# Four blocks on one core: merged attention weights in the third, projections in three rounded terms, joined rows, and a new order

## The chip, the cores and the metric

One core of a Trainium2 chip runs the whole program. The metric is device time in microseconds (us) of one execution.

## The reference

The program computes four blocks in a row on an activation of 2048 tokens by 256 channels, handled as four batches of 512 tokens. Each block normalises its input and adds two branches to it:

```python
xn = _layernorm(x); x = x + L0_attn(xn) + L0_ffn(xn)   # causal attention, 16 heads of 16; ternary feed-forward, 1024 units
xn = _layernorm(x); x = x + L1_attn(xn) + L1_ffn(xn)   # gated recurrence; 16 experts by top 2 with slots, and a shared expert of 176
xn = _layernorm(x); x = x + L2_attn(xn) + L2_ffn(xn)   # attention, one head of 256; spline-coded feed-forward, 1024 units
xn = _layernorm(x); x = x + L3_attn(xn) + L3_ffn(xn)   # attention with rope, 16 heads; 8 experts in bf16, shared expert of 176, plus xn

q = x@wq.T; k = x@wk.T; v = x@wv.T                     # L2_attn
out = softmax(q@k.T / sqrt(256)) @ v @ wo.T
logits = x @ gate_w.T                                  # L1_ffn, 16 columns; L3_ffn has the same with router_w, 8 columns
shared = (act(x@Ws1.T) * (x@Ws3.T)) @ Ws2.T            # L1_ffn and L3_ffn, act is silu and sigmoid
```

## The kernel before, in words

The code numbers the blocks k = 0 to 3. A batch b has four token tiles of 128. Every matrix product runs on TensorE (PE) into PSUM: three pairs of banks used in a ring ("pair") and two single banks.

Every engine executes its own list of steps in an order that is written out by hand. `PARTS` names the steps of each engine, `DUE` gives each step a turn, and `Turns` sorts by turn. Nothing is reordered while the program runs: a step that waits holds up all later steps of its engine. `freed` (L485) makes PE wait, before it fills a bank, until the readers named in `FREED` are done with what was in it.

Products come in three kinds. Plain fp32 operands are issued by PE as two matmul records each, so the counts of the trace are twice those of the code. Operands rounded to fp32r take one record; the feed-forward layers of blocks 0 and 2 use these with a high part and a low part that sum to the fp32 value (`cut_high`, `cut_low`, `h_high`, `h_low`, `w_in2`, `w_out2`). Block 3's experts run in bf16.

A batch of a block starts with the layer norm (`stat`, `norm` on VectorE, DVE), eight transposes (`turn_x`, L618), and a copy of the result from PSUM by ScalarE, ACT (`turned`, L1520: to `xnT`, in blocks 0 and 2 also rounded to `cut_high`; `cut_low` on DVE, L1029, subtracts that). Blocks 0 and 3 then project a token tile in one step, `qkv` (L627): two fp32 products of 512 columns, two of 256. Head groups follow: `fold`, `score`, `top` (row maxima on DVE), `refold`, `prob`, `exp` (ACT), `weigh`, with feed-forward steps between them in the hand-written order. Block 1 projects with `proj`, computes gates, a scan and two group norms mostly on DVE, and routes with `logit` (L825), `route_a` to `route_e` and `count`; its experts follow. Block 2 is `qk2` (L872, queries and keys apart), `v2`, `score2`, `probs_turn`, `weigh2` (L904, probabilities times values), and the output product with `wo2` in `out` (L715), where the feed-forward sum joins. Block 3's router is `vote` (L912). `shared` (L815) computes the gate and up columns of the shared expert in two steps, the 128 first and the 48 last columns, each with two products per half. At the start, twelve chunks of ternary weights are made by ACT, PE, DVE and GpSimd (POOL) in turn (`tern_*`). Between blocks 1 and 2 the spline weights are made (`cubic`, `spline`, `spline_sum`). Loads are issued by SyncE (SP) in the order of `load`. `quarter` (L983) scales the query weights and bias of blocks 0 and 3 by 0.25.

## Time and profile before

| what | value |
|---|---|
| device time, median of 3 runs | 1569.27 us (1563.61 to 1571.36) |
| the profiled execution: its time / its span | 1562.3 us / 1561.0 us |
| PE busy, share of the span | 1336.0 us, 86% |
| DVE busy | 946.1 us, 61% |
| ACT busy | 680.3 us, 44% |
| POOL busy | 412.9 us, 26% |
| mean granted clock of TensorE | 0.91 of full |

The profile is one execution. Busy time is the time that an engine spent in instructions; a clock of 1.00 is 2.4 GHz and 0.50 is 1.2 GHz. The duration of one matmul includes its way through the array, so the pace of a row of matmuls is read from the distance between starts.

### The profile page before, as it was taken

How to read it: one execution, taken by the hardware profiler on the slowest of the kernel's cores; microseconds unless marked ns; L12 is line 12 of the kernel's file. 1: busy time of each engine (PE TensorE's matmuls, PEld its weight loads, DVE VectorE, ACT ScalarE, POOL GpSimd, SP SyncE). 2: the span in 40 equal slices, each digit the busy share in tenths (PEclk: the TensorE clock that was granted, in tenths of full speed). 3: DMA queues.
4: the chain of work that ended last, by engine and by line, in shares of the span. 5: the costliest groups of instructions: out<-in, count | busy, mean ns of one | idle time of the engine just before them, and what ended most of it. 6: DMA issues, size and time to landing. Idle time of an engine off the chain costs nothing.

```text
span 1561.0 us, 19705 instructions
## 1 busy us (share of the span) xinstructions
PE 1336.0 (86%) x7705; PEld 810.8 (52%) x7716; DVE 946.1 (61%) x1822; ACT 680.3 (44%) x960; POOL 412.9 (26%) x397
## 2 busy tenths in 40 slices
PE   0589999999999668889469999999899898988997
PEld 0367666776654335445146677676445335434434
DVE  5895563584557999882586234346675765556560
ACT  3435555444664755442024224231463453453452
POOL 2465000541002331410662122133223302301300
PEclk9979996899999889899579999999799899989978
DMA  7000000004010000025550000000311000200100
GB/s 227 14 1 1 1 2 1 1 1 150 22 45 28 27 24 4 27 75 165 155 81 0 1 1 1 8 17 1 61 42 38 17 0 1 54 1 1 55 1 14
DMA packets 32012, 53.21 MB, mean 34 GB/s; under 512 B 5200, under 2 KB 19760, under 8 KB 31280
## 3 DMA queue, kind: packets, MB, share of 16 engines
q1 hardware_dynamic: 27840, 40.99, 8.5%
q0 software_dynamic: 4080, 10.97, 3.3%
q8 instruction: 61, 1.00, 0.3%
q14 instruction: 31, 0.25, 0.1%
HBM read 43.99 MB, written 10.52 MB: 35 GB/s over the span
## 4 chain that ended last, share of the span: by engine, by line
PE 45%; DVE 27%; issue 15%; ACT 5%; POOL 5%; DMA 1%; SPq 1%; DVEq 0%; POOLq 0%; ACTq 0%
PE pair L609 15%; PE bank L609 14%; DVE max L1094 6%; PE bank L692 4%; PE pair L680 3%; PE pair L642 3%; ACT probs L1580 2%; PE pair L660 2%; POOL cos L1885 1%; DVE xn L1026 1%; POOL square_sum L1902 1%; POOL gathered L1934 1%; DMA gathered<-outbox,slots 1%; SPq L1966 1%; DVE tern_mask L973 1%
## 5 line engine op out<-in xcount | busy, mean ns | idle before, releaser
L1094 DVE TENSOR_REDUCE max<-pair 128x2 f32<-128x1024 f32 (+3 forms) x256 | 245.9, 1015 | 85.3 <-PE pair L650 51.9
L1580 ACT ACTIVATE probs<-pair 128x1024 f32<-128x1024 f32 (+3 forms) x256 | 206.9, 871 | 128.9 <-PE pair L650 78.3
L1892 POOL TENSOR_TENSOR h_low<-hidden,h_high 128x512 fp32r<-128x512 f32 x64 | 82.4, 1288 | 262.3 <-ACT h_high L1615 262.3
L692 PE MATMUL bank<-probs,v 128*32 128x512 f32 (+3 forms) x1024 | 131.4, 590 | 2.5 <-ACT probs L1580 2.2
L680 PE MATMUL pair<-qs,ks 52*128 52x512 f32 (+3 forms) x512 | 110.8, 480 | 24.1 <-DVE max L1094 13.1
L660 PE MATMUL pair<-ks,qs 50*128 50x512 f32 (+3 forms) x512 | 115.9, 480 | 16.9 <-DVE max L1094 7.0
L680 PEld LDWEIGHTS pair<-qs,ks 52*128 52x128 f32 x512 | 50.5, 207 | 106.7 <-issue 37.0
L609 PE MATMUL pair<-wqk,xnT 128*128 128x512 f32 x192 | 98.3, 637 | 3.0 <-DVE tern_what L981 2.6
L1144 DVE SCALAR_TENSOR_TENSOR hidden<-hidden,pair 128x512 f32<-128x512 f32 x64 | 43.7, 683 | 82.5 <-ACT hidden L1607 82.5
L1952 POOL TENSOR_TENSOR h<-mix_h,h 128x512 bf16<-128x512 f32 x48 | 55.4, 1168 | 133.8 <-DMA h<-comb 78.8
L660 PEld LDWEIGHTS pair<-ks,qs 50*128 50x128 f32 x512 | 52.3, 205 | 71.1 <-DVE max L1094 30.8
L1607 ACT ACTIVATE hidden<-pair 128x512 f32<-128x512 f32 x64 | 38.2, 597 | 106.3 <-PE pair L609 106.0
L1127 DVE TENSOR_TENSOR x<-bank,x 128x512 f32<-128x512 f32 x32 | 21.9, 686 | 101.3 <-PE bank L609 101.3
L609 PE MATMUL bank<-wo,rowsT 128*128 128x256 f32 x256 | 70.7, 405 | 10.2 <-DVE x L1127 2.4
L642 PE MATMUL pair<-ident_r,stack 128*128 128x128 f32 x512 | 57.3, 272 | 13.2 <-POOL stack L1861 9.1
L1615 ACT CAST h_high<-hidden 128x512 fp32r<-128x512 f32 x64 | 39.4, 619 | 66.6 <-DVE hidden L1146 52.5
L1857 POOL CAST stack<-raw 128x256 fp32r<-128x256 f32 x32 | 13.8, 430 | 201.7 <-DVE stack L1085 201.7
L642 PEld LDWEIGHTS pair<-ident_r,stack 128*128 128x128 f32 x512 | 51.7, 151 | 24.2 <-issue 14.5
L609 PEld LDWEIGHTS bank<-wo,rowsT 128*128 128x128 f32 x256 | 46.1, 196 | 26.8 <-issue 8.6
L609 PE MATMUL pair<-xnT,shared_in 128*48 128x512 f32 (+1 forms) x128 | 59.7, 612 | 0.1
L1563 ACT CAST qs<-pair 128x1024 fp32r<-128x1024 f32 x32 | 32.5, 1017 | 56.9 <-PE pair L642 56.8
L609 PE MATMUL pair<-x,w_in 128*128 128x512 bf16 x181 | 51.6, 426 | 6.0 <-DVE mix_h L1494 3.1
(293 smaller groups left out, 2823.8 us busy)
## 6 DMA issues: line engine op xcount, KB each, us to landing
expert_in<-in_experts_in SPq DMA_DIRECT2D x16, 352.0 KB, 3.8
expert_out<-in_experts_out SPq DMA_DIRECT2D x16, 256.0 KB, 5.1
h<-comb SPq DMA_DIRECT2D x4, 1024.0 KB, 5.0
x<-in_x SPq DMA_DIRECT2D x4, 512.0 KB, 11.2
wqk<-in_wqk SPq DMA_DIRECT2D x4, 512.0 KB, 3.9
tern_raw<-in_ffn_in SPq DMA_DIRECT2D x8, 256.0 KB, 6.5
inbox<-zeros SPq DMA_DIRECT2D x4, 512.0 KB, 5.3
tokens<-inbox SPq DMA_DIRECT2D x16, 128.0 KB, 2.5
```

The lines of the kernel that those rows point to most:

```text
L609: made = mm(out, lhsT, rhs, start=start and n == 0, stop=stop and n == len(pairs) - 1)
L642: made = turn(to[:, p, tt * P:(tt + 1) * P].bitcast(F32R), m.stack[g % 2][:, tt, half, 2 * p:2 * p + 2, :].rearrange("p h r -> p (h r)"), ...
L660: made = mm(to[:, hh, 0:n], m.qs[g % 2][r0:r0 + AUG + 2, p, qt * P:(qt + 1) * P], m.ks[g % 2][r0:r0 + AUG + 2, p, 0:n], start=True, stop=k ...
L680: made = mm(to[:, hh, q0:T], m.ks[g % 2][r0:r0 + AUG + 4, p, kt * P:(kt + 1) * P], m.qs[g % 2][r0:r0 + AUG + 4, p, q0:T], start=True, stop ...
L692: made = mm(to[32 * j:32 * j + 32, q0:T], m.v[b % 2][:, kt, G * g + j, :], m.probs[(2 * kt + j // 2) % 4][:, j % 2, q0:T], start=kt == 0, ...
L1094: V.tensor_reduce(m.max[:, g % 2, qt, 2 * p:2 * p + 2], to[:, :, 0:n], AX.X, ALU.max).then_inc(*s.done("top"))
L1144: V.scalar_tensor_tensor(h[:, :], h[:, :], 1.0, to[:, 0, :], ALU.add, ALU.mult).then_inc(*dve.up())
L1580: A.activation(m.probs[(2 * kt + p) % 4][:, :, q0:T], to[:, :, q0:T], ACT.Exp).then_inc(*s.done("exp"))
L1607: A.activation(m.hidden[k][j % 2][:, :], to[:, 0, :], ACT.Tanh, scale=0.5).then_inc(*s.done("tanh"))
L1615: A.copy(m.h_high[k][:, j, :], m.hidden[k][j % 2][:, :]).then_inc(*s.done("high"))
L1892: Q.tensor_tensor(m.h_low[k][:, j, :], m.hidden[k][j % 2][:, :], m.h_high[k][:, j, :].bitcast(F32), ALU.subtract).then_inc(*s.done("low"))
L1952: Q.tensor_tensor(m.h16[:, j, :], m.mix_h[j % 2][:, :], m.h16[:, j, :], ALU.mult).then_inc(*s.done("mix_comb"))
```

## The change

- Block 2 (the third): the host hands over the four raw weight matrices. Two new PE steps `merge` multiply wq by wk and wv by wo once; ACT and DVE split each result into a high and a low part. `qk2` becomes one step for a batch, a product of the input with the merged matrix, and `score2` multiplies it with the input itself. `v2` uses the other merged matrix. `weigh2`, `weighed2` and the product with wo are gone; `out` multiplies the probabilities with `v2` directly.
- Three rounded terms (`three`: high·high, low·high, high·low) replace each fp32 product in `qkv` of blocks 0 and 3, `qk2`, `v2`, `score2`, and `shared` of block 3. New steps `split_high` (ACT) and `split_low` (POOL) split the weights. Block 3 now has a `cut_low` too, and its `x16` copy is part of `turned`.
- `shared` in both blocks: the 48 last gate and up columns sit in one product of 112 columns instead of two of 48.
- `logit` and `vote` are gone: the router's 16 or 8 columns are added to the value projection (272 or 264 columns), with a small copy to SBUF by ACT (block 1) or DVE (block 3).
- `quarter` is gone; the factor 0.25 moves into `exp` (ACT's scale), and the host scales `k_extra` by 4.
- Nearly all turns in `DUE` are new, among them those of the loads, and several tiles lie elsewhere in SBUF.

The diff, cut to its core (`layout` on the host, most turn lists and addresses are left out):

```diff
-    "score2": "639 644 645 653 656 659 663 667 688 693 694 701 706 711 712 717",
+    "score2": "638 634 639 644 661 662 657 666 686 687 683 679 705 710 706 701",
...
-    "load": "0 1 3 2 5 6 7 4 8 17 23 24 33 35 34 76 77 9 83 82 84 85",
+    "load": "1 7 6 0 5 2 8 4 9 17 23 24 33 34 35 76 3 81 82 83 84",
...
-    "turn": lambda k, b: [("turned", (k, b))] + [("cut_low", (k, b))] * (k in (0, 2)),
+    "turn": lambda k, b: [("turned", (k, b))] + [("cut_low", (k, b))] * (k != 1),
...
+    "merge": lambda i: [("merge_high", (i,)), ("merge_low", (i,))],
+    "qk2": lambda b: [("qk2_out", (b,)), ("qk2_low", (b,))],
...
+    def three(x, w):
+
+        return [(x[0], w[0]), (x[1], w[0]), (x[0], w[1])]
...
     def qkv(k, b, tt):
         to = bank("qkv", k, b, tt)
-        pe.wait_ge(*at("turned", k, b))
-        pe.wait_ge(*s.loaded(f"qkv{k}"))
-        pe.wait_ge(*at("quarter", k))
-        xT = [m.turned(k, b)[:, kc, tt * P:(tt + 1) * P] for kc in range(KC)]
-        products(to[:, 0, :], [(xT[kc], m.wqk[k][:, kc, :]) for kc in range(KC)])
-        products(to[:, 1, 0:C], [(xT[kc], m.wv[k][:, kc, :]) for kc in range(KC)]).then_inc(*s.done("qkv"))
+        pe.wait_ge(*at("cut_low", k, b))
+        pe.wait_ge(*at("split_high", k // 3))
+        pe.wait_ge(*at("split_low", k // 3))
+        for part, high, low in ((0, m.wqk_high[k], m.wqk_low[k]), (1, m.wv_high[k], m.wv_low[k])):
+            pairs = [pair for kc in range(KC) for pair in three([x[:, kc, tt * P:(tt + 1) * P] for x in (m.high(k, b), m.cut_low)], [high[:, kc, :], low[:, kc, :]])]
+            made = products(to[:, part, 0:low.shape[2]], pairs)
+        made.then_inc(*s.done("qkv"))
...
-            pe.wait_ge(*at("weighed2", b))
+            pe.wait_ge(*s.last("v2_out", [(b, half) for half in PAIRS]))
+            pe.wait_ge(*s.last("probs_out", [(b, 2 * i + n) for n in PAIRS]))
...
-            made = products(to[:, cols], [(m.rowsT[k][:, kc, tok], m.wo[k][:, kc, :]) for kc in range(KC)], stop=k == 0)
+            if k == 2:
+                products(to[:, cols], [(m.probsT[:, kt, tok], m.v2[b % 2][:, kt, :]) for kt in range(TT)], stop=False)
+            else:
+                made = products(to[:, cols], [(m.rowsT[k][:, kc, tok], m.wo[k][:, kc, :]) for kc in range(KC)], stop=k == 0)
...
-        products(to[:, 1, 0:C], [(xT[kc], m.wv1[:, kc, :]) for kc in range(KC)]).then_inc(*s.done("proj"))
+        products(to[:, 1, 0:C + E1], [(xT[kc], m.wv1[:, kc, :]) for kc in range(KC)]).then_inc(*s.done("proj"))
...
     def shared(k, b, c):
         to = bank("shared", k, b, c)
-        pe.wait_ge(*at("turned", k, b))
-        pe.wait_ge(*s.loaded("rest1" if k == 1 else "shared3"))
-        n_rows = (P, I - P)[c]
-        for part in PAIRS:
-            c0 = part * I + c * P
-            made = products(to[0:n_rows, part, :], [(m.shared_in[k][:, kc, c0:c0 + n_rows], m.turned(k, b)[:, kc, :]) for kc in range(KC)])
+        if k == 1:
+            pe.wait_ge(*at("turned", k, b))
+            pe.wait_ge(*s.loaded("rest1"))
+        else:
+            pe.wait_ge(*at("cut_low", k, b))
+            pe.wait_ge(*at("split_high", 2))
+            pe.wait_ge(*at("split_low", 2))
+        for part, cols in enumerate(((slice(0, P), slice(P, 2 * P)), (slice(2 * P, SHARED),))[c]):
+            if k == 1:
+                pairs = [(m.shared_in[1][:, kc, cols], m.turned(b)[:, kc, :]) for kc in range(KC)]
+            else:
+                pairs = [pair for kc in range(KC) for pair in three([m.shared_high[:, kc, cols], m.shared_low[:, kc, cols]], [m.high(3, b)[:, kc, :], m.cut_low[:, kc, :]])]
+            made = products(to[0:(P, SMALL)[c], part, :], pairs)
         made.then_inc(*s.done("shared"))
-
-    def logit(b):
-        to = bank("logit", b)
-        pe.wait_ge(*at("turned", 1, b))
-        pe.wait_ge(*s.loaded("rest1"))
-        for tt in range(TT):
-            made = products(to[:, tt * E1:(tt + 1) * E1], [(m.turned(1, b)[:, kc, tt * P:(tt + 1) * P], m.wroute1[:, kc, :]) for kc in range(KC)])
-        made.then_inc(*s.done("logit"))
...
-    def qk2(b, half):
-        to = bank("qk2", b, half)
-        pe.wait_ge(*at("turned", 2, b))
+    def merge(i):
+
+        to = bank("merge", i)
         pe.wait_ge(*s.loaded("qkv2"))
         for mc in range(KC):
-            c0 = half * C + mc * P
-            made = products(to[:, mc, :], [(m.wqk[2][:, kc, c0:c0 + P], m.turned(2, b)[:, kc, :]) for kc in range(KC)])
+            made = products(to[:, mc * C:(mc + 1) * C], [(m.raw2[:, 2 * i, kc, mc * P:(mc + 1) * P], m.raw2[:, 2 * i + 1, kc, :]) for kc in range(KC)])
+        made.then_inc(*s.done("merge"))
+
+    def qk2(b):
+        to = bank("qk2", b)
+        pe.wait_ge(*at("cut_low", 2, b))
+        pe.wait_ge(*at("merge_high", 0))
+        pe.wait_ge(*at("merge_low", 0))
+        for mc in range(KC):
+            pairs = [pair for kc in range(KC) for pair in three([w[:, kc, mc * P:(mc + 1) * P] for w in m.merged[0]], [x[:, kc, :] for x in (m.cut_high, m.cut_low)])]
+            made = products(to[:, mc, :], pairs)
         made.then_inc(*s.done("qk2"))
     def v2(b, i):
         to = bank("v2", b, i)
-        pe.wait_ge(*at("turned", 2, b))
-        pe.wait_ge(*s.loaded("qkv2"))
+        pe.wait_ge(*at("cut_low", 2, b))
+        pe.wait_ge(*at("merge_high", 1))
+        pe.wait_ge(*at("merge_low", 1))
         for n in PAIRS:
             tok = slice((2 * i + n) * P, (2 * i + n + 1) * P)
-            made = products(to[:, n * C:(n + 1) * C], [(m.turned(2, b)[:, kc, tok], m.wv[2][:, kc, :]) for kc in range(KC)])
+            pairs = [pair for kc in range(KC) for pair in three([x[:, kc, tok] for x in (m.cut_high, m.cut_low)], [w[:, kc, :] for w in m.merged[1]])]
+            made = products(to[:, n * C:(n + 1) * C], pairs)
         made.then_inc(*s.done("v2"))
     def score2(b, qt):
         to = bank("score2", b, qt)
-        pe.wait_ge(*at("qk2_out", b, 0))
-        pe.wait_ge(*at("qk2_out", b, 1))
-        qk = m.qk2[b % 2]
-        products(to[:, :], [(qk[:, 0, kc, qt * P:(qt + 1) * P], qk[:, 1, kc, :]) for kc in range(KC)]).then_inc(*s.done("score2"))
+        pe.wait_ge(*at("qk2_out", b))
+        pe.wait_ge(*at("qk2_low", b))
+        pairs = [pair for kc in range(KC) for pair in three([q[:, kc, qt * P:(qt + 1) * P] for q in m.qk2[b % 2]], [x[:, kc, :] for x in (m.cut_high, m.cut_low)])]
+        products(to[:, :], pairs).then_inc(*s.done("score2"))
...
-    def quarter(k):
-        dve.wait_ge(*s.loaded(f"bias{k}"))
-        dve.wait_ge(*s.loaded(f"qkv{k}"))
-        V.tensor_scalar(m.bias[k][:, 0, :], m.bias[k][:, 0, :], 0.25, None, ALU.mult).then_inc(*dve.up())
-        V.tensor_scalar(m.wqk[k][:, :, 0:C], m.wqk[k][:, :, 0:C], 0.25, None, ALU.mult).then_inc(*s.done("quarter"))
...
         to = bank("turn", k, b)
         dve.wait_ge(*at("turned", k, b))
-        V.tensor_tensor(m.cut_low[:, :, :], to[:, :, :], m.cut_high[:, :, :].bitcast(F32), ALU.subtract).then_inc(*s.done("cut_low"))
+        if k == 3 and b == 0:
+            dve.wait_ge(*s.last("unit", [(2, BATCH - 1, j) for j in range(UNITS)]))
+            dve.wait_ge(*s.last("score2", [(BATCH - 1, qt) for qt in range(TT)]))
+            dve.wait_ge(*s.last("v2", [(BATCH - 1, i) for i in PAIRS]))
+        elif k == 3:
+            dve.wait_ge(*s.last("qkv", [(3, b - 1, tt) for tt in range(TT)]))
+            dve.wait_ge(*s.last("shared", [(3, b - 1, c) for c in PAIRS]))
+        V.tensor_tensor(m.cut_low[:, :, :], to[:, :, :], m.high(k, b).bitcast(F32), ALU.subtract).then_inc(*s.done("cut_low"))
...
+    def merge_low(i):
+        to = bank("merge", i)
+        dve.wait_ge(*at("merge_high", i))
+        V.tensor_tensor(m.merged[i][1][:, :, :], to[:, :].rearrange("p (k c) -> p k c", k=KC), m.merged[i][0][:, :, :].bitcast(F32), ALU.subtract).then_inc(*s.done("merge_low"))
+
+    def qk2_low(b):
+        to = bank("qk2", b)
+        dve.wait_ge(*at("qk2_out", b))
+        V.tensor_tensor(m.qk2[b % 2][1][:, :, :], to[:, :, :], m.qk2[b % 2][0][:, :, :].bitcast(F32), ALU.subtract).then_inc(*s.done("qk2_low"))
...
+        if k in (0, 2) and b > 0:
+            act.wait_ge(*s.last("unit", [(k, b - 1, j) for j in range(UNITS)]))
+        if k == 2 and b > 0:
+            act.wait_ge(*s.last("score2", [(b - 1, qt) for qt in range(TT)]))
+            act.wait_ge(*s.last("v2", [(b - 1, i) for i in PAIRS]))
...
+        A.copy(m.high(k, b), to[:, :, :]).then_inc(*(act.up() if k == 3 else s.done("turned")))
+        if k == 3:
             if b > 0:
-                act.wait_ge(*s.last("unit", [(k, b - 1, j) for j in range(UNITS)]))
-            elif k == 2:
-                act.wait_ge(*s.last("finish", [(b2, h, last) for b2 in B for h in PAIRS for last in PAIRS]))
-                act.wait_ge(*at("route_e", BATCH - 1))
-                for b2 in B:
-                    act.wait_ge(*s.sent(b2))
-                act.wait_ge(*s.last("weighted", [(b2, h, last) for b2 in B for h in PAIRS for last in PAIRS]))
-                act.wait_ge(*s.last("count", [(b2,) for b2 in B]))
-            A.copy(m.cut_high[:, :, :], to[:, :, :]).then_inc(*s.done("turned"))
+                act.wait_ge(*s.last("mix", [(b - 1, j) for j in range(MIX)]))
+            else:
+                act.wait_ge(*at("probs_turn", BATCH - 1, 0))
+            A.copy(m.x16[:, :, :], to[:, :, :]).then_inc(*s.done("turned"))
+
+    def split_high(n):
+
+        k = (0, 3, 3)[n]
+        act.wait_ge(*s.loaded(("qkv0", "qkv3", "shared3")[n]))
+        if n == 1:
+            act.wait_ge(*s.last("combine", [(b, tt) for b in B for tt in range(TT)]))
+        if n == 2:
+            A.copy(m.shared_high[:, :, :], m.shared_in[3][:, :, :]).then_inc(*s.done("split_high"))
+            return
+        A.copy(m.wqk_high[k][:, :, :], m.wqk[k][:, :, :]).then_inc(*act.up())
+        A.copy(m.wv_high[k][:, :, :], m.wv[k][:, :, :]).then_inc(*s.done("split_high"))
...
+    def split_low(n):
+
+        k = (0, 3, 3)[n]
+        pool.wait_ge(*at("split_high", n))
+        for w, high, low_ in ((m.shared_in[3], m.shared_high, m.shared_low),) if n == 2 else ((m.wqk[k], m.wqk_high[k], m.wqk_low[k]), (m.wv[k], m.wv_high[k], m.wv_low[k])):
+            Q.tensor_tensor(low_[:, :, :], w[:, :, :], high[:, :, :].bitcast(F32), ALU.subtract).then_inc(*(pool.up() if w.shape[2] == 2 * C else s.done("split_low")))
...
-    def weigh2(b):
...
-    def vote(b):
...
-    def weighed2(b):
...
-    def x16(b):
...
```

## Rows read from the trace of the kernel before

**Rows 1.** The page: busy us of each engine, share of the span, instructions.
```profile
PE 1336.0 (86%) x7705; PEld 810.8 (52%) x7716; DVE 946.1 (61%) x1822; ACT 680.3 (44%) x960; POOL 412.9 (26%) x397
```

**Rows 2.** Stages: stretch, length, busy PE, PEld, DVE, ACT, POOL; clock, DMA share, GB/s.
```profile
0.00:120.00 120.00, 60.55 (x296) 41.09 (x297) 96.14 (x178) 45.66 (x71) 55.69 (x55) 0.90 0.27 79
120.00:462.00 342.00, 324.46 (x2998) 225.76 (x2997) 186.27 (x349) 179.38 (x266) 77.93 (x96) 0.92 0.08 25
462.00:745.00 283.00, 235.95 (x874) 133.97 (x872) 219.89 (x505) 141.75 (x210) 69.35 (x58) 0.92 0.15 49
745.00:800.00 55.00, 21.88 (x60) 9.80 (x61) 36.87 (x62) 9.14 (x14) 34.74 (x33) 0.54 0.50 125
800.00:1056.00 256.00, 245.64 (x1093) 176.50 (x1091) 116.24 (x239) 80.24 (x133) 68.41 (x53) 0.99 0.07 12
1056.00:1561.00 505.00, 447.51 (x2392) 223.65 (x2403) 290.67 (x494) 224.16 (x266) 106.75 (x105) 0.90 0.08 22
```

**Rows 3.** The page: the chain that ended last, by engine.
```profile
PE 45%; DVE 27%; issue 15%; ACT 5%; POOL 5%; DMA 1%; SPq 1%; DVEq 0%; POOLq 0%; ACTq 0%
```

**Rows 4.** Timeline, PE: 8 fp32 records of 512 columns and what follows.
```profile
818.93 3.59 PE L609 MATMUL pair<-xnT,wqk 128*128 128x512 f32 x8
821.96 1.03 PE L609 MATMUL pair<-cut_high,w_in_high 128*128 128x512 f32 x2
822.82 0.39 PE L609 MATMUL pair<-cut_high,w_in_low 128*128 128x512 f32 x1
```

**Rows 5.** Timeline, PE: rounded products of 512 columns, 16 between the two starts.
```profile
805.01 0.63 PE L609 MATMUL pair<-cut_high,w_in_low 128*128 128x512 f32 x2
...
808.68 0.62 PE L609 MATMUL pair<-cut_high,w_in_high 128*128 128x512 f32 x2
```

**Rows 6.** Timeline, PE: 16 fp32 records of 256 columns.
```profile
986.20 3.61 PE L609 MATMUL bank<-wv,xnT 128*128 128x256 f32 x16
989.65 1.88 PE L609 MATMUL bank<-qk 128*128 128x512 f32 x4
```

**Rows 7.** Timeline, PE: rounded products of 256 columns.
```profile
874.15 1.12 PE L609 MATMUL bank<-w_out_high,h_low 128*128 128x256 f32 x8
...
876.07 1.03 PE L609 MATMUL bank<-wo,rowsT 128*128 128x256 f32 x4
```

**Rows 8.** Timeline, PE: one `logit` and one `vote`, each with the next row.
```profile
463.84 1.86 PE L609 MATMUL bank<-wroute,xnT 128*128 128x16 f32 x16
465.54 1.96 PE L609 MATMUL pair<-wqk,xnT 128*128 128x512 f32 x4
...
1132.04 1.95 PE L609 MATMUL bank<-wroute,xnT 128*128 128x8 f32 x16
1133.92 0.73 PE L660 MATMUL pair<-ks,qs 50*128 50x512 f32 x4
```

**Rows 9.** PE's waits in block 2 and in block 3: us in total, times, longest.
```profile
PE bank L901 <- DVE probs L1448: 7.1, 7, 1.9
...
PE pair L680 <- DVE max L1094: 11.3, 20, 1.7
```

**Rows 10.** Durations in ns (min/median/max): the high copy, the low cut.
```profile
L1555 ACT CAST cut_high<-pair x8: 1016/1018/1037, 56.0 to 973.4; 128x1024 fp32r<-128x1024 f32 x8
L1032 DVE TENSOR_TENSOR cut_low<-pair,cut_high x8: 1210/1216/1225, 60.5 to 974.5; 128x1024 fp32r<-128x1024 f32 x8
```

**Rows 11.** Timeline, start: ACT's first ternary cast, DVE's first norm, PE's first `qkv`.
```profile
21.13 0.62 ACT L1515 CAST tern_w<-tern_raw 128x512 bf16<-128x512 f32 x1 [19.11 <-DMA tern_raw<-in_ffn_in]
42.35 0.42 DVE L1006 BATCH_NORM_STATS2 stats<-x 128x6 f32<-128x256 f32 x1
60.64 3.78 PE L609 MATMUL pair<-wqk,xnT 128*128 128x512 f32 x4 [2.62 <-DVE tern_what L981]
```

**Rows 12.** Slices of the head-group stretch of block 0 at either clock.
```profile
190.00:200.00 10.00, 9.20 (x122) 5.71 (x121) 6.61 (x11) 5.41 (x9) 0.88 (x3) 1.00 0.01 2
...
240.00:250.00 10.00, 10.00 (x88) 5.73 (x86) 7.05 (x12) 2.62 (x4) 0.00 (x0) 0.50 0.01 2
```

More of the change, by code:

```diff
@@ L956, in set_dve @@
             dve.wait_ge(*s.last("unit", [(2, BATCH - 1, j) for j in range(UNITS)]))
-            dve.wait_ge(*s.last("weigh2", [(b,) for b in B]))
+            dve.wait_ge(*s.last("score2", [(b, qt) for b in B for qt in range(TT)]))
         for tile_ in m.v:
@@ L1056, in rope_a @@
             dve.wait_ge(*s.last("low", [(2, BATCH - 1, j) for j in range(UNITS)]))
-            dve.wait_ge(*s.last("weigh2", [(b2,) for b2 in B]))
         if (b, tt) >= (0, 2):
```

276 lines of the change are left out of this document (138 added, 138 removed), and 281 rows, old and new, of the table DUE.

## The prediction

> **What bounds the kernel now.** I read the page first. PE is busy 1336.0 of 1561.0 us, the next engine 946.1 [rows 1], and the chain that ended last is 45% PE and 27% DVE, with 15% "issue" [rows 3]. The page averages over stages, so the second view is the table of stages [rows 2]; the reader should compare PE's busy time with each stretch's length.
> - 0 to 120 (start, first batches of block 0): DVE 96.1, PE 60.6. DVE bounds it.
> - 120 to 462 (block 0): PE 324.5 of 342. PE bounds it.
> - 462 to 745 (block 1 and its experts): PE 236, DVE 220 of 283; neither alone.
> - 745 to 800 (spline weights): PE 21.9 of 55, a chain of small steps.
> - 800 to 1056 (block 2): PE 245.6 of 256, clock 0.99. Pure PE.
> - 1056 to 1561 (block 3): PE 447.5 of 505, DVE 290.7.
>
> So PE time that is removed should come back nearly whole in block 2, mostly in blocks 3 and 0, and in small part in block 1.
>
> **Prices.** An fp32 record of 512 columns: from 818.93 to 822.82 lie eight of them and two rounded products [rows 4]. A rounded product of 512 columns is (808.68 − 805.01)/16 = 0.229 us [rows 5], so the eight take 3.89 − 0.46 = 3.43, 0.429 each, and an fp32 product (two records) 0.858. An fp32 record of 256 columns is (989.65 − 986.20)/16 = 0.216 us [rows 6], a rounded product of that width (876.07 − 874.15)/16 = 0.120 [rows 7]. Three rounded terms hence cost 0.687 against 0.858 at 512 columns, 0.360 against 0.431 at 256: a fifth and a sixth less, no more.
>
> **The change on PE, by block.**
> - `qkv`, 16 tiles a block: before 4 × 0.429 + 4 × 0.216 = 2.58, after 6 × 0.229 + 6 × 0.120 = 2.09. 0.49 × 16 = 7.8 us in block 0. In block 3 the eight added columns cost 0.12 × 8/256 × 96 = 0.4, which leaves 7.4.
> - `shared`, four batches: before 16 records, 6.86 us. Block 3 after: two products of 128 columns and one of 112, six terms each, 18 × 0.229 = 4.12; saves 2.74 × 4 = 11.0. Block 1 stays fp32 with three quarters of the records: 1.72 × 4 = 6.9.
> - `logit`: 16 records in 465.54 − 463.84 = 1.70 us, × 4 = 6.8; `vote`: 1.88 × 4 = 7.5 [rows 8]. The 16 columns in `proj` cost 4 × 0.013 × 16 tiles = 0.9.
> - `qk2`: 16 records, 6.86, become 12 rounded products, 2.75: 4.11 × 4 = 16.5. `v2`: 16 × 0.216 = 3.45 to 24 × 0.120 = 2.88: 2.3. `score2`: 6.86 to 24 × 0.229 = 5.50: 5.4. `weigh2` and wo: 16 × 0.429 + 16 × 0.216 = 10.3 become 32 records of 256, 6.9: 13.7.
> - `merge`, added: 16 records of 256 in all, 3.5 us, or 6.9 at half clock. They stand among the spline steps, where PE is idle for 33 of 55 us [rows 2], so I cost them at nothing; without that cover they cost their 3.5 to 6.9.
>
> By block that is 7.8, 12.8, 37.9 and 25.9, in all 84.4 us of PE.
>
> **What of it reaches the end.** Block 2: 37.9, less two things. Projections now wait for the high copy and the low cut, 1.02 + 1.22 [rows 10], where `v2` waited only for a copy; at the first batch nothing covers this, about 1.3 us. A batch's `turned` now also waits for the `score2` of the batch before, because the single `cut_high`/`cut_low` serve as keys; behind it on ACT stand the tanh and high copies of the units, and PE waits for these. In the new order PE has `out` of the last batch between the two, some 9 us of work, so I charge only growth of the softmax wait, now 7.1 us over seven times [rows 9], by 0 to 7, and take 2.5. Credit 34.
>
> Block 0: half of its `qkv` tiles stand in the DVE-bound start, the rest under a busy PE. The bounds are 3.9 and 7.8; I take 5, nearer the PE-bound half. At the start the new order takes batch 0's statistics before the first ternary chunk. DVE does them at 42.35 now, while everything waits for data until 21.13 [rows 11]. x0 is now loaded behind x2, x1, the projection weights and the biases, still before the ternary chunks. Some 2 us of DVE work moves into the gap and `quarter` goes; against it stand `split_high` and `split_low`, 1.6 us on ACT and about 4 on POOL (from `cut_high`'s 1.02 per 1024 elements [rows 10]; POOL's side I bound by 2 to 6), in front of POOL's first ternary product. Bounds −3 to +4 for the start, taken as a gain of 2.
>
> Block 1: DVE has 220 busy us of 283, and nothing of note leaves DVE (`route_a`'s four small copies), while ACT gains 16 small ones. Between none and all of 12.8, I take 5.
>
> Block 3: 25.9, of which the waits for row maxima (11.3 us [rows 9]) and the DVE side take a part. DVE gains four cuts of 1.22 and 16 vote copies, about 7 us on an engine that is idle 214 us there. The new `cut_low` is a single buffer and holds the transposes' PSUM pair through two ACT copies and the cut, 3.3 us instead of 1; with three pairs in the ring, at worst 2.3 × 4 = 9 us. It waits for the last `qkv` and `shared` of the batch before, which the new turns put far ahead. Credit between 10 and 26, taken as 18.
>
> The spline stage keeps its length; its first two loads change places, ±3.
>
> Sum: 34 + 5 + 2 + 5 + 18 = 64 us. The profiled execution took 1562.3, of which the span is 1561.0, so it would be 1498. The median shown, 1569.27, lies 7 above it; repeated runs scatter by 8, so I add 5: **1503 us**.
>
> **A page on the pace.** Rounded products come every 0.229 us here [rows 5]. The Trainium skill ("TensorE: Matmul & The Clock Gate", section "Back-to-back issue gap") gives about 131 ns for a sustained stream of 512 columns with weight loads. By it the 408 new products of that width would cost 0.098 less each, 40 us in all, and the time would be 1463. The trace has over 380 of this very pattern in block 2 and none at that pace, so the row decides.
>
> **Rivals.**
> 1. *Only block 2 gives.* Blocks 0, 1 and 3 are held by latencies between DVE, ACT and PE, and a lighter PE waits longer for maxima. For it: PE's DVE waits in block 3 [rows 9], DVE 27% of the chain [rows 3]. Against it: PE busy 95% in block 0 and 89% in block 3 [rows 2]. Gain about 30: 1537.
> 2. *More than the sum.* The new order also closes gaps: PE is idle 225 us in all [rows 1]. All 84 and some 15 of gaps: 1472.
> 3. *Slower, by the clock.* A head-group slice at 1.2 GHz gets through 88 records in 10 us, one at 2.4 GHz through 122 [rows 12]: 2.8 us are lost in ten. The mean clock of 0.91 says that 18% of the span, 281 us, ran at the low level. The dense projections between the head groups become shorter, so PE's short pauses weigh more. If the low share doubled (mean clock 0.82), 281 × 0.28 = 79 us would be lost: 1503 + 79 = 1582. It cancels the gain from a mean clock of 0.84 down. Against it: block 2 keeps 0.99 at 96% busy, and the head groups, where the low stretches lie, do not change. The Trainium skill (same page, section "A second HAM failure mode: psum-queue depth-cycling") says that short pauses between matmul groups throw the clock back; by that rule the price is the one just worked out.
> 4. *Nothing gained:* the new turns are badly placed, and steps held in order eat what the sum saves; within 8 us of 1569.
>
> **How the numbers follow.** Forecast 60%, rival 1 20%, rival 2 9%, rival 3 6%, rival 4 5%. The forecast's own range is 1482 to 1525 (credits of 85 to 42). To hold 8 in 10 I go from 1468, rival 2, to 1541, rival 1 with a little less. This kernel's measurement tells from no change what lies over 0.5%, 8 us. Faster by more: 60 + 20 + 9 = 89%. Same: 5%. Slower: 6%.
>
> **What would show each step.** Block 2 from its first `v2` to its last `out` shrinks by 30 to 40 us with PE still over 93% busy. Three rounded terms in `qkv` take about 2.1 us a tile. PE's busy total falls to about 1250. Block 1 shrinks by under 8. If PE's waits on maxima in block 3 grow by 10 or more and that block shrinks by less than 10, rival 1 holds there. If rounded products of 256 columns run slower than 0.120 where the weights are 264 or 272 wide, `qkv` gives nothing. A mean clock below 0.87 would mean rival 3 at work. The prediction is wrong if block 2 does not shrink, or if the first `qkv` starts later than 60.6 us.

## The result and the profile after

The changed kernel takes **1503.19 us** (median of 4 runs, 1501.14 to 1510.51) against 1570.32 for the kernel before beside it, a ratio of 0.958 (95% interval 0.9525 to 0.9634). The forecast was 1503.0. A hit to 0.2 us is luck: over its ten runs the changed kernel's median is 1504.4, and 1505.7 in the second session alone. That the total is right says little about its terms, so the rest of this document asks which of them are.

The page of the changed kernel, busy time of each engine and the chain that ended last, to be laid beside [rows 1] and [rows 3]:
```profile
PE 1244.3 (83%) x7757; PEld 809.6 (54%) x7772; DVE 976.6 (65%) x1840; ACT 668.8 (45%) x967; POOL 420.9 (28%) x402
...
PE 33%; DVE 22%; issue 6%; ACT 5%; POOL 2%; DMA 1%; SPq 0%; DVEq 0%; POOLq 0%
```
PE lost 91.7 us of busy time (84.4 were worked out), DVE gained 30.5; 11.6 of these are one product of block 3 that now runs blocked by POOL (last section). The stages, cut at the changed kernel's own marks, with the columns of [rows 2]:
```profile
0.00:120.00 120.00, 57.16 (x282) 42.66 (x284) 94.26 (x172) 42.91 (x69) 58.55 (x56) 0.87 0.26 79
120.00:440.00 320.00, 305.21 (x3069) 221.68 (x3069) 189.28 (x351) 179.57 (x265) 80.05 (x97) 0.97 0.08 27
440.00:707.00 267.00, 213.79 (x772) 119.13 (x766) 218.96 (x500) 143.37 (x226) 68.51 (x53) 0.90 0.16 50
707.00:779.00 72.00, 38.96 (x107) 19.68 (x105) 43.14 (x65) 9.77 (x16) 41.40 (x39) 0.62 0.42 108
779.00:986.00 207.00, 199.28 (x1080) 172.78 (x1081) 113.71 (x231) 65.05 (x115) 65.61 (x50) 0.98 0.07 11
986.00:1502.00 516.00, 429.93 (x2460) 233.66 (x2473) 317.27 (x523) 228.16 (x276) 106.75 (x108) 0.89 0.08 23
```
Read from the two timelines, the stretches between the same steps are:

| stretch | before, us | after, us | difference |
|---|---|---|---|
| start to first `proj` (start, block 0) | 460.7 | 440.2 | −20.5 |
| to the last `expert_out` (block 1) | 275.6 | 267.1 | −8.5 |
| to the first `v2` (spline stage) | 62.1 | 71.6 | +9.5 |
| to the end of the last `out` of block 2 | 296.1 | 245.4 | −50.7 |
| to the end (block 3) | 466.4 | 477.6 | +11.1 |

These are two single executions. In a second profile of the changed kernel (experiment 11) the stretches are 440.9, 267.7, 70.9, 246.4 and 469.7: four of them repeat within 1 us, block 3 does not, and its +11.1 would be +3.3. The sum is −59.1, but hardly a line is what the forecast says (−7, −5, 0, −34, −18). Either the prices of the work are wrong and the errors cancel, or something else moves time from stage to stage. The records speak for the prices. A `qkv` tile of block 3, PE's timeline:
```profile
1002.37 0.39 PE L617 MATMUL pair<-wqk_high,cut_low 128*128 128x512 f32 x1
1002.60 0.39 PE L617 MATMUL pair<-wqk_low,xnT_high 128*128 128x512 f32 x1
1002.83 0.40 PE L617 MATMUL pair<-wqk_high,xnT_high 128*128 128x512 f32 x1
...
1003.53 0.28 PE L617 MATMUL pair<-wv_high,xnT_high 128*128 128x264 f32 x1
...
1004.25 0.39 PE L617 MATMUL pair<-wqk_high,xnT_high 128*128 128x512 f32 x1
```
Starts lie 0.23 us apart at 512 columns and (1004.25 − 1003.53)/6 = 0.12 at 264, and the next tile takes 2.10 us: the prices of [rows 5] and [rows 7]. The rule weighed in the forecast, 131 ns in a sustained stream (the Trainium skill, "TensorE: Matmul & The Clock Gate", section "Back-to-back issue gap"), is borne out by no row of this kernel either.

### The profile page after: what moved, and what is told of

The parts are those of the page before. It is cut to its first block, busy times and chain, and to the rows that moved or that the text cites. A ratio compares the mean times of both kernels' runs of the same rounds, so it can differ in the third digit from the quotient of the medians.

```text
span 1501.9 us, 19793 instructions
## 1 busy us (share of the span) xinstructions
PE 1244.3 (83%) x7757; PEld 809.6 (54%) x7772; DVE 976.6 (65%) x1840; ACT 668.8 (45%) x967; POOL 420.9 (28%) x402
## 4 chain that ended last, share of the span: by engine, by line
PE 33%; DVE 22%; issue 6%; ACT 5%; POOL 2%; DMA 1%; SPq 0%; DVEq 0%; POOLq 0%
PE pair L617 11%; PE bank L617 11%; DVE max L1113 4%; PE bank L705 3%; ACT probs L1620 3%; PE pair L673 2%; PE pair L693 2%; POOL inbox L1967 1%; DVE conv L1194 1%; PE pair L655 1%; DVE xn L1032 1%; DVE sin L1081 1%; DVE x L1412 1%; DVE normed L1286 1%; DVE mix_h L1517 1%
## 5 line engine op out<-in xcount | busy, mean ns | idle before, releaser
L1113 DVE TENSOR_REDUCE max<-pair 128x2 f32<-128x1024 f32 (+3 forms) x256 | 250.8, 1019 | 90.4 <-PE pair L673 54.5
L705 PE MATMUL bank<-probs,v 128*32 128x512 f32 (+3 forms) x1024 | 127.3, 572 | 5.0 <-ACT probs L1620 4.8
L693 PE MATMUL pair<-qs,ks 52*128 52x512 f32 (+3 forms) x512 | 104.3, 454 | 24.9 <-DVE max L1113 4.5
L1899 POOL CAST stack<-raw 128x256 fp32r<-128x256 f32 x32 | 13.7, 428 | 201.1 <-DVE stack L1104 201.1
L1517 DVE SCALAR_TENSOR_TENSOR mix_h<-mix_t,pair 128x512 f32<-128x512 f32 x48 | 32.4, 684 | 49.7 <-ACT mix_t L1849 49.5
L617 PE MATMUL bank<-wo,rowsT 128*128 128x256 f32 x192 | 54.5, 416 | 6.3 <-ACT rowsT L1636 3.1
L1849 ACT ACTIVATE mix_t<-pair 128x512 f32<-128x512 f32 x48 | 29.0, 606 | 66.1 <-PE pair L617 65.9
L1926 POOL TENSOR_TENSOR cos<-raw,rope 128x512 f32<-128x512 f32 x16 | 21.1, 1319 | 110.4 <-DVE raw L1055 101.4
L1967 POOL DMA_INDIRECT inbox<-xn,route_slots x32 | 35.4, 1106 | 55.8 <-DVE slots L1390 47.3
```

The lines of the kernel that those rows point to most:

```text
L617: made = mm(out, lhsT, rhs, start=start and n == 0, stop=stop and n == len(pairs) - 1)
L693: made = mm(to[:, hh, q0:T], m.ks[g % 2][r0:r0 + AUG + 4, p, kt * P:(kt + 1) * P], m.qs[g % 2][r0:r0 + AUG + 4, p, q0:T], start=True, stop ...
L705: made = mm(to[32 * j:32 * j + 32, q0:T], m.v[b % 2][:, kt, G * g + j, :], m.probs[(2 * kt + j // 2) % 4][:, j % 2, q0:T], start=kt == 0, ...
L1113: V.tensor_reduce(m.max[:, g % 2, qt, 2 * p:2 * p + 2], to[:, :, 0:n], AX.X, ALU.max).then_inc(*s.done("top"))
L1517: V.scalar_tensor_tensor(h, m.mix_t[j % 2][:, :], 1.0, to[:, 1, :], ALU.add, ALU.mult).then_inc(*s.done("mixed"))
L1967: Q.indirect_dma_start(inbox[:, :], bass.IndirectOffsetOnAxis(ap=m.r["slots"][:, tt, k:k + 1], axis=0), m.normal(1, b)[:, tt, :], None).th ...
```

## The experiments

Two kinds are used. In one the old PE work of a block is put back into the changed kernel, whose order and waits stay; in the other the order alone is changed. One reading helps with all: each run comes with the mean clock granted to it. Over the 120 runs of all kernels here, each kernel taken about its own mean, a run is 1.07 us longer for every thousandth that its clock is lower. For the kernel before that is 21 of the 28 us between its extremes, 1552.8 (0.917) and 1581.2 (0.897). [Rows 12] give the same size: a thousandth of mean clock is 0.002 × 1561 = 3.1 us at the low level, at 0.28 lost in each, 0.9 us. So below a median stands with a second number, the mean of the runs brought to a clock of 0.908: **1565.3 before, 1500.5 after** (48 runs and 10 runs, standard errors 0.3 and 0.5).

**1. Order of the start and of block 0, undone.**
```
 DUE: start and block 0 in the old relative order on every engine, the rest new
+sp.wait_ge(*s.last("qkv", [(0, BATCH - 1, tt) for tt in range(TT)]))   # vec1
```


> The changed kernel with its work untouched, but the start and block 0 in the relative order of the kernel before on every engine (loads, ternary chunks, statistics, units, head groups), the rest in the new order. The first proj of block 1 came at 460.8 us before and comes at 440.2 after, 20.6 earlier, where the forecast gave 7. Theory (the new turns close gaps there, the lighter qkv gives under 8): first proj moves back to 452 to 457, first qkv to about 60, total 1515 to 1520. Rival (the lighter qkv shortens the stretch and with it the low-clock time, the turns do nothing): first proj stays within 4 us of 440, total 1500 to 1506. Rival 2 (the turns are the whole of it, the lighter qkv gives nothing): first proj back at 460, total about 1524.


Measured: 1534.12 (1529.56 to 1545.04; at 0.908: 1524.4). First `qkv` and first `proj` here, in the order after, old order:
```profile
53.12 0.79 PE L617 MATMUL pair<-wqk_high,cut_high 128*128 128x512 f32 x1 [3.75 <-DVE cut_low L1045]
...
440.21 1.98 PE L617 MATMUL pair<-wqk,xnT 128*128 128x512 f32 x4
```
```profile
64.64 0.77 PE L617 MATMUL pair<-wqk_high,cut_high 128*128 128x512 f32 x1 [3.80 <-DVE cut_low L1045]
...
453.43 1.98 PE L617 MATMUL pair<-wqk,xnT 128*128 128x512 f32 x4
```
The splits and the wait for the low cut delay the first `qkv` by 4.0 (60.64 in [rows 11] to 64.64); the new order brings it 11.5 forward. At the first `proj` the order is worth 13.2, the lighter work the other 7.3. But the total rose by 30, more than expected: block 1 behind the seam took 285.1 us instead of 267.1. Most of that is one wait. PE's first routing product of block 1, in the order after and here:
```profile
465.77 0.20 PE L617 MATMUL bank<-route_load,earlier 128*128 128x16 bf16 x1 [2.06 <-DVE route_weight L1360]
```
```profile
488.86 0.17 PE L617 MATMUL bank<-route_load,earlier 128*128 128x16 bf16 x1 [13.54 <-DVE route_weight L1360]
```
In the order after, the four first `proj` stand in a row, and the routing's DVE steps begin at 453.8. Here gates, heads and `gamma` stand between them, the fourth `proj` comes at 472.4, and the routing begins at 478.1.

**2. Block 2's PE work put back.**
```
-pairs = [... three(merged[0], (cut_high, cut_low))]
+pairs = [... plain(merged[0], cut_high)]     # plain fp32, issued twice in qk2
 v2, score2: three(...) -> plain(...)
+products(to[:, 0:C], [(probsT[:, kt, tok0], v2[:, kt, :]) for kt in range(TT)])   # in out
```


> The changed kernel in its own order, with block 2's old PE time put back as plain fp32 products of the high parts and repeated products whose result is overwritten (the low parts' terms are left out): qk2 16 fp32 records of 512 a batch, v2 16 of 256, score2 16 of 512, and 16 of 256 more ahead of out. By the forecast's prices that is 37.9 us in all. Block 2, from its first v2 to the last out, took 244.2 us after against 294.9 before, 50.7 less. Theory (PE alone bounds block 2, so removed work comes back one for one, and the other 13 are out steps that stood behind the first folds of block 3 and small waits): block 2 grows by 35 to 39, total 1538 to 1542. Rival (the new terms are cheaper than priced): it grows by 45 to 50, total 1548 to 1553. Rival 2 (part of the work hides under the softmax waits): it grows by less than 30.


Measured: 1531.99 (1523.72 to 1541.4; at 0.908: 1532.5). The stretch v2 to last `out` after, and with the work back, each in two parts (length, PE, PEld, DVE, ACT, POOL):
```profile
778.90:985.40 206.50, 198.74 (x1077) 172.55 (x1078) 113.51 (x231) 65.05 (x115) 65.72 (x50) 0.98 0.07 11
985.40:1024.40 39.00, 36.12 (x223) 31.82 (x221) 33.22 (x72) 7.61 (x13) 15.35 (x12) 1.00 0.05 17
```
```profile
778.40:1013.90 235.50, 231.64 (x1078) 178.50 (x1079) 113.10 (x231) 64.89 (x115) 65.69 (x50) 0.99 0.05 10
1013.90:1055.00 41.10, 39.92 (x237) 34.52 (x235) 34.94 (x75) 7.60 (x13) 16.68 (x15) 1.00 0.05 17
```
PE's busy time grows by 36.7 where 37.9 was priced, the stretch by 31.1, so 5.6 us vanish in waits: PE's wait for the softmax weights falls from 6.7 to 2.6. The forecast credited 34; the work gives 31.1 in the stretch, 32.0 at one clock and 27.6 by the medians, less than the 35 to 39 of this run's theory, since a part hides in the softmax waits. The other 19.6 of the 50.7 aren't block 2's work. With the old work of all blocks put back (experiment 12) the stretch takes 282.1, 5.5 more than here: the projections of block 3's first batch stand in it. The last 14.0 belong to the order. PE's busy time in the stretch is 277.2 there and 283.7 in the kernel before, so about 6 of the 14 are work that left the stretch for block 3; the rest are waits, 5.0 instead of 12.4.

**3. Block 3's PE work put back.**
```
 qkv (k == 3), shared (k == 3): three(...) -> plain(...)
+products(to[0:SMALL, 1, :], pairs)           # shared, c == 1: a fourth product
+16 fp32 records of 8 columns (the votes)
```


> The changed kernel in its own order, with block 3's old PE time put back: qkv and shared as plain fp32 products of the high parts (the low parts' terms are left out), one shared product and the votes' 16 small fp32 records repeated into columns that nothing reads. By the forecast's prices 25.9 us of PE. From the last unit of block 2 to the end the kernel got 9.5 us longer where the forecast had it 18 shorter. Theory (PE work is worth about 0.7 of its time here, and the new turns and the single cut_low cost the rest): total 1503 + 16 to 21 = 1519 to 1524. Rival (block 3 is held by maxima, the light PE only waits longer): total 1503 to 1509. Rival 2 (all of it on the path): 1529.


Measured: 1525.87 (1515.01 to 1530.82; at 0.908: 1520.9), 21.5 above the changed kernel's 1504.4 (median of its 10 runs), 20.4 at one clock. The theory's 16 to 21 holds at its upper edge; the rival with maxima falls, and so does the one with all 25.9 on the path.

**4. The merges ahead of the spline steps.**
```
 PE:  merge0, merge1 before spline01;  ACT: merge_high0 first
 SP, DVE: spline_load0, cubic0 before spline_load1, cubic1
```


> The changed kernel with both merges on PE ahead of the first spline product, in the time when PE waits for the spline loads (715.8 to 729.3), the merge's high copy ahead of the first spline's, and the first spline load and its cubic in front of the second. From the first spline product to the first v2 it takes 49.6 us after and 41.1 before; the two merges stand in it with 3.8 us each at half clock. Theory (they are on the path, as the forecast said they would be without their cover): this stretch shrinks by 7 to 8, the first spline starts within 2 us of 729.3, total 1494 to 1497. Rival (the stretch is held by DVE and the gathers, the merges are hidden): it shrinks by less than 2, total 1501 to 1504. Rival 2 (raw2 arrives late and the merges now delay the first spline): first spline later by 4 or more, nothing gained.


Measured: 1495.64 (1491.22 to 1499.9; at 0.908: 1496.9). PE in the changed kernel, then here:
```profile
731.16 1.92 PE L887 MATMUL pair<-cubics,powers 32*128 32x512 f32 x4
...
764.72 3.78 PE L617 MATMUL bank<-raw 128*128 128x256 f32 x8
```
```profile
719.64 6.45 PE L617 MATMUL bank<-raw 128*128 128x256 f32 x16 [5.67 <-DMA raw<-in_raw]
726.01 1.13 PE L886 MATMUL pair<-cubics,powers 16*128 16x512 f32 x4
```
In the changed kernel each merge takes 3.8 us between spline steps that wait for one another. Moved, they fill 6.45 us of a wait. The stage from last `expert_out` to first `v2` is 68.0 us, against 71.6 and 70.9 in two profiles of the changed kernel: 3 to 4 us, half of what the theory said, and 3.6 at one clock. First spline to first `v2` shrinks only by 2.1, about as its rival has it; the rest came from the earlier first spline.

**5. The new order of start and block 0 in the kernel before.**
```
 DUE of the kernel before: start and block 0 in the new relative order, the rest old
```


> The mirror of the run with the old turns: the kernel before with its work untouched, but the start and block 0 in the new relative order (new load order, statistics before the first ternary chunk), the rest in the old one. Undoing the turns in the changed kernel moved its first qkv from 53.1 to 64.6 us and its first proj from 440.2 to 453.4. Theory (the turns are worth 11 to 13 us wherever they are used): first qkv at 50 to 52, first proj at 446 to 450 instead of 460.7. Rival (they only pay together with the lighter qkv, which makes PE late less often): first proj within 4 us of 460.7.


Measured: 1564.79 (1561.66 to 1571.02, ratio 0.9991, 0.9958 to 1.0024; at 0.908: 1569.8). The first `qkv` comes at 50.6, the first `proj` at 445.95, 14.8 earlier, so the theory's mechanism is shown a second time. The total doesn't move: block 1 takes 288.9 us instead of 275.6 and eats it.

**6 and 7. The PE work of blocks 0 and 1 put back.**
```
 6: qkv (k == 0): three(...) -> plain(...)
 7: shared (k == 1, c == 1): +products(to[0:SMALL, 1, :], pairs), +16 fp32 records of 16 columns
```


> The changed kernel in its own order with block 0's qkv as plain fp32 products of the high parts (the low parts' terms are left out), all waits kept: 16 tiles of 2.58 instead of 2.09 us by the forecast's prices, 7.8 us of PE. Theory (PE-bound stretch, the share of it under the DVE-bound start is lost): first proj of block 1 moves from 440.2 to between 444 and 448, total 4 to 8 above 1503. Rival (a heavier PE lifts the clock and the work costs nothing): first proj stays within 2 us.

> The changed kernel in its own order with block 1's old PE work put back in `shared`: a fourth product of 512 columns (1.72 us a batch) and the 16 small fp32 records of the logits (1.70 a batch), written to columns that nothing reads; 13.7 us of PE in all. From the first proj to the last expert_out it took 275.6 us before and 265.0 after. Theory (a third of it shows, the rest lies beside DVE and the latencies, as the forecast's 5 of 12.8): the stretch grows by 3 to 7. Rival (PE-bound): by 12 to 14. Rival 2 (nothing of it shows, the 10.6 came from the turns): by less than 2.


Measured: 1508.82 (1504.28 to 1511.98; at 0.908: 1505.0) and 1507.49 (1504.22 to 1510.87; at 0.908: 1507.0). With block 0's work the first `proj` comes at 448.6, 8.4 later, all of the 7.8, but only 4.5 reach the end. With block 1's, its stretch is 274.1 against 267.1 (267.7 in the changed kernel's second profile): it grows by 6.4 to 7.0 of the 13.7 put back, at the theory's upper edge, and 3 to 6.5 reach the end.

**8. Block 3's `qkv` and `shared` ahead of both last outs.**
```
 PE:  turn30, qkv30*, shared30*, out231, fold30*, out230, scores
 DVE: top231, norms, cut_low30, weight231, set_dve3; cuts before vote_b
```


> The kernel with the early merges (1495.6), and besides the first batch of block 3 in another order. In the changed kernel DVE spends 989.4 to 995.5 on the four clears of set_dve before it cuts the first low part, PE does a whole out (9.3 us) and waits for the last softmax weight before the first qkv at 1002.1; from there to the end of the first sixteen maxima lie 48.6 us, exactly as many as before (1063.6 to 1112.2), since DVE bounds it. Now the last softmax maximum and the low cut go ahead of the clears, qkv and shared ahead of both outs, the folds' cuts ahead of the routing. Theory (the DVE chain of the first batch is what the new turns delayed): first qkv comes 5 to 9 us sooner after the last unit, first store 5 to 8 sooner, total 1487 to 1491. Rival (the clock falls in the maxima phase as before and eats it): the first store gains under 2 us, total 1494 to 1497.


Measured: 1512.56 (1499.89 to 1517.94; at 0.908: 1503.2), 6 worse at one clock than the kernel it builds on. The folds come 9 us earlier as planned, but the last two outs of block 2 now stand behind them or among them, and DVE, in order, waits with `joined230` ahead of its maxima:
```profile
1025.04 0.69 DVE L1146 TENSOR_TENSOR x<-bank,x 128x512 f32<-128x512 f32 x1
...
1035.26 0.69 DVE L1146 TENSOR_TENSOR x<-bank,x 128x512 f32<-128x512 f32 x1 [8.85 <-PE bank L617]
...
1038.84 1.23 DVE L1113 TENSOR_REDUCE max<-pair 128x2 f32<-128x1024 f32 x1 [0.88 <-PE pair L673]
```
The 9 us went into a new wait of 8.85: the first sixteen maxima end 69.8 us after the last unit, against 66.7 in experiment 4. Neither theory had it.

**9. Scores issued twice where PE waits for maxima.**
```
+for again in range(2 if k == 3 and b == 0 and g < 2 else 1):
     made = mm(to[:, hh, 0:n], ...)
```


> The changed kernel in its own order; in block 3's first batch the score products of the first two head groups are issued twice (same operands, same output), 16 scores of two products more, while PE waits for the row maxima that DVE takes one every 1.14 us. From 1023 to 1154 us the granted clock is 0.83 and before it was 0.89 in the like stretch, and that stretch grew by 19 us. Theory (the pauses of the maxima phase drop the clock, and the low level costs the head groups after it; a busier PE keeps it up): mean clock of that stretch rises to 0.87 or more, the first store comes 3 to 8 us sooner than 168.6 us after the last unit, total 1495 to 1500. Rival (the clock does not hang on these pauses, or a doubled score at the low level takes longer than a maximum): the first store comes 3 to 10 us later, total 1505 to 1513.


Measured: 1496.57 (1494.55 to 1503.59; at 0.908: 1499.7), ratio 0.9604 (0.9563 to 0.9645) beside 0.9651 (0.9621 to 0.968) for the changed kernel on the same chip. At one clock that is 0.5 to 0.8 less than the changed kernel, nothing beyond the noise. In the profile the first sixteen maxima end 2.3 us later after the last unit than in the changed kernel's (67.4; 65.1 and 65.2), so the 32 products more are cheap under the maxima, though not free. The clock from 37.4 to 168.4 us after the last unit is 0.87, the theory's mark, but it is 0.87 in experiment 11 too, without the doubled scores (0.83 in the changed kernel's first profile). The theory isn't shown, and the intervals overlap.

**10 and 11. A better version, and the changed kernel beside it.**
```
 experiment 4, and: POOL: root20 before spline_low21
 DVE: top231, norms, cut_low30, weight231 before set_dve3; cuts before vote_b0, shared_out300
```


> The kernel with the early merges, and two small moves more. POOL takes block 2's first root ahead of three low products: in the kernel with early merges DVE's 0.17 us scaling of the variances ran 3.91 us beside them. At the start of block 3 PE keeps the changed kernel's order, and on DVE the last softmax maximum, the norms, the low cut and the last weight go ahead of the four clears, the folds' cuts ahead of the routing. Theory (both stood on the path): last expert_out to first v2 falls from 68.0 to 63 to 65 us, last unit to first fold from 42.7 to 38 to 41, total 1486 to 1491. Rival (DVE has other work in both places and the chain keeps its length): both stretches within 1 us of those, total 1494 to 1497.

> The changed kernel itself once more, beside these two on one chip, so that differences of a few us can be told. 1500 to 1507 by every theory; the stretches of block 1 (265.0 us from first proj to last expert_out) and of block 3 (516.5 from last unit to the end) tell how much a stretch scatters from one profile to the next.


Measured: **1490.78** (1488.13 to 1493.85; at 0.908: 1492.0; ratio 0.9549, 0.952 to 0.9577) beside 1505.74 (1496.82 to 1509.58). The intervals are apart: 15 us by the medians, 8.5 at one clock. Last unit to first fold fell from 41.2 to 36.4, and to the end of the first sixteen maxima from 65.1 to 60.0. In the spline stage DVE's small scaling and POOL beside it, in experiment 11 and in experiment 10:
```profile
761.96 3.92 DVE L1020 TENSOR_SCALAR rstd<-moments 128x4 f32<-128x4 f32 x1
...
762.14 1.27 POOL L1983 TENSOR_TENSOR w_in_low<-spline_raw,w_in_high 128x512 fp32r<-128x512 f32 x1
763.36 1.26 POOL L1983 TENSOR_TENSOR w_out_low<-spline_raw,w_out_high 128x512 fp32r<-128x512 f32 x1
764.59 1.25 POOL L1983 TENSOR_TENSOR w_in_low<-spline_raw,w_in_high 128x512 fp32r<-128x512 f32 x1
```
```profile
761.96 0.17 DVE L1020 TENSOR_SCALAR rstd<-moments 128x4 f32<-128x4 f32 x1
...
762.21 1.21 POOL L1893 TENSOR_TENSOR rstd<-rstd,minus_half 128x4 f32<-128x4 f32 x1
```
The stall of 3.75 us is gone, but 2.2 of it came back at once, as a wait for the next spline's products on PE, and the stage took 67.0 where 63 to 65 were expected: the rival was right there.

**12. All the old work at once, in the new order.**


> The changed kernel with all of block 0's to block 3's old PE work put back at once, as in the four runs that did one block each (the low parts' terms are left out; repeated products are overwritten or land in columns that nothing reads), its new turns, splits, cuts and merges kept. Read at one mean clock (a thousandth of it is worth 1.08 us over all runs so far), the changed kernel stands at 1500.5 us for 0.908, the kernel before at 1565.4, and the four put back 4.5, 6.5, 32.0 and 20.4, 63.4 in all. Theory (the work alone makes the gain, the terms add up, and the turns win 13 in block 0 and lose as much later): 1559 to 1569 at 0.908, no different from the kernel before. Rival (the turns are worth their 13 to 15 of block 0 in the end too): 1545 to 1553. Rival 2 (put-back work costs more together than alone): above 1573.


Measured: 1567.65 (1560.64 to 1572.22, 12 runs), ratio to the kernel before **1.000** (0.9965 to 1.0036). PE is busy 1332.3 us, against 1336.0 in [rows 1]: the work is back. By the medians it costs 63.2 us. Its clock is higher, 0.914 in the mean against 0.907 for the kernel before beside it, and at 0.908 it stands at 1573.0, 7.7 above the kernel before. By the scale that was set for this run the theory (1559 to 1569) missed, and the result lies at the edge of rival 2, work that costs more together than alone (72.5 against 63.4). So the time is the same to within 6 us, but it is made of 8 us more at one clock and a clock that gives them back. Whether this order earns the higher clock is not shown. PE's load doesn't explain it: the kernel before has the same busy time and 0.907, and experiments 4 and 10 have the changed kernel's work and 0.909 against 0.904.

## Why the prediction was right

**The work, by block.** What each block's work is worth at the end, by putting it back:

| block | PE work | forecast | by medians | at 0.908 |
|---|---|---|---|---|
| 0 | 7.8 | 5 | 4.4 | 4.5 |
| 1 | 12.8 | 5 | 3.1 | 6.5 |
| 2 | 37.9 | 34 | 27.6 | 32.0 |
| 3 | 25.9 | 18 | 21.5 | 20.4 |
| sum | 84.4 | 62 | 56.6 | 63.4 |
| all at once | 84.4 | 62 | 63.2 | 72.5 |

(Medians against the 1504.4 of the changed kernel's ten runs; with four runs each an entry is good to some 3 us. For block 1, 13.7 us were put back.) So the whole work is worth 63 by the medians, the size that the forecast credited, and 72 at one clock. The credits of blocks 1, 2 and 3 (under half, nearly whole, seven tenths) came from PE's share of each stage in [rows 2], 83%, 96% and 89%, and they hold. At one clock they measure 0.47, 0.84 and 0.79 of the work put back. Inside block 2, the softmax wait for which 2.5 us were charged did not grow against the kernel before (6.7 for 7.1); with the old work put back it is 2.6, so the new order had shrunk it and the lighter work gave 4.1 back. Block 0's credit holds for another reason than the forecast gave: in its own stretch, 95% PE, the work shows whole (8.4 for 7.8, the DVE-bound start hides none of it), and about half doesn't reach the end. Where it goes is not shown; block 1, the spline stage and block 2 behind it take the same time as in the changed kernel, within about 1 us.

**The order: right in sum, wrong in place.** The step that failed is the term of the start, "taken as a gain of 2"; its bounds of −3 to +4 failed with it. The new order brings the first `qkv` 11.5 us forward, the new steps take 4.0 back. Beside the lighter work it is worth 13.2 at the first `proj` (14.8 in the kernel before). The spline stage "keeps its length" failed too: it grew by 9, by the merges in the chain (3 to 4, experiment 4, at the lower end of the 3.5 to 6.9 named for a missing cover), a DVE operation held up by POOL (net 1, experiment 10), and about 4 not told apart. All of this cancels: with the old work in the new order the kernel is as fast as before to within 6 us. The forecast had reckoned with neither size, so that they cancel is luck. Stage by stage, one profile each, that kernel stands to the one before at −8 (to the first `proj`), −2 (block 1), +6 (spline), −14 (block 2) and +26 (block 3). About 6 of block 2's 14 only move a boundary (experiment 2): before, the folds of block 3, 2.9 us, and its first scores stood ahead of the last `out`.

**Block 3's start.** The work saved 14 (from the last unit on, one profile) to 21 us, and yet the stretch from last `out` grew by 11 (3 in the second profile). One cause is seen. Before, PE did `vote`, `shared` and `qkv` right behind the last unit; in the new order it does an `out` of 9.3 us and waits for the last softmax weight, which stands on DVE behind the clears of `set_dve`:
```profile
989.38 1.76 DVE L971 MEMSET v<- 128x2048 f32 x1 [1.33 <-PE bank L617]
991.52 1.76 DVE L971 MEMSET v<- 128x2048 f32 x1 [0.38 <-issue]
993.66 1.76 DVE L972 MEMSET stack<- 128x2048 f32 x1 [0.38 <-issue]
...
995.54 1.19 DVE L1045 TENSOR_TENSOR cut_low<-pair,xnT_high 128x1024 fp32r<-128x1024 f32 x1
...
999.54 1.99 DVE L1472 TENSOR_SCALAR probs<-probs,total 128x512 f32<-128x512 f32 x1
```
From the last unit to the end of the first sixteen maxima it takes 65.3 us instead of 58.2. From the first `qkv` on it is 48.6 in both kernels, but that is a coincidence: with block 3's old work put back (experiment 3) it is 51.8, so the lighter `qkv` and `shared` gave 3, and the order took them. Experiment 10, which moves the last maximum, the low cut and the last weight ahead of the clears and the folds' cuts ahead of the routing, brings the 65 down to 60, so DVE's order there is shown as the cause of 5 us. Behind it, up to the first store, 103.3 (clock 0.88) and 99.8 (0.93) in two profiles of one kernel, 92.7 (0.95) before; the clock explains the difference of the two, not that to before. PE's waits over block 3 show the single `cut_low` at work:
```profile
PE pair L693 <- DVE cut_low L1045: 3.6, 2, 2.4
PE pair L617 <- DVE cut_low L1045: 2.3, 1, 2.3
```
These 5.9 us didn't exist before, and they stand in the profiles of experiments 10, 11 and 12 as well; the forecast had allowed up to 9 for them. PE's waits for `mix_h` grew from 4.6 to 11 us and those for ACT's `probs` from 4 to 10. How much of this reaches the end was not tried: the old order can't be had with the single `cut_low` and `x16`, since a batch's `turned` waits for the last `mix` of the one before.

**The rivals.** Rival 1 fell: PE's waits for maxima in block 3 grew from 16.3 to 18.3 (`score` and `prob` together), not by 10, and the three blocks outside block 2 gave about what was credited. Rival 2's gaps were closed in block 0 and opened again later. Rival 3, the clock, is there at a small part of its 79 us: the mean over all runs fell from 0.9075 to 0.9043, 3.4 us. On the one chip that ran both with the clocks on record (experiment 11) it fell from 0.9124 to 0.9040, 9 us. Of the signs named ahead, `qkv` at 2.1 us a tile, PE at 1250 and its share in block 2 (96%) came true; "block 2 shrinks by 30 to 40" and "block 1 by under 8" did not, as marks between two kernels of unequal order, and did as experiments.

## What to carry to other kernels

Where work and order change together, the lengths of the stages of the two kernels don't tell what the work was worth: put the work back, block by block, in the new order, and once all of it. A credit by PE's share of the stage (96%: nearly whole, 89%: seven tenths, 83%: under half) was good to 3 us a block at one clock and to 6 by the medians. In a kernel whose clock wanders, compare runs at one mean clock before reading 5 us as an effect, and say so when the clock itself differs from kernel to kernel, as in experiment 12. Mark the ends of a stage at the same event in both kernels, and take a second profile before a stage's difference is believed: block 3 alone moved by 8 us from one profile to the next. And a step that is moved forward, as in experiment 8, first has to be followed through the in-order queue of the engine that takes its result.
